# Loading a layer's weights ahead of the second tile's activations in the feed-forward groups of an attention and quantized-FFN kernel

## What is computed

```python
def _dequant(q, scale):
    return (q / 7.5 - 1.0) * repeat(scale, 16, axis=1)

def _qlora_linear(x, q, scale, bias, la, lb):
    base = einsum('btd,od->bto', x, _dequant(q, scale)) + bias
    return base + einsum('btr,or->bto', einsum('btd,rd->btr', x, la), lb)

h = x
for blk in range(3):
    y = _qlora_linear(h, qweights[2*blk], ...)
    y = gelu(_layernorm(y, ...))
    y = _qlora_linear(y, qweights[2*blk+1], ...)
    h = y + h
out = _layernorm(x + h)
```

## Time and profile before

| | us |
|---|---|
| median of two timed runs | 2959.98 (2907.43 to 3012.53) |
| the profiled execution | 2838.79 |
| its span, from first to last instruction on the slowest core (7) | 2837.3 |
| spans of the eight cores | 2818.8 to 2837.3 |
| TensorE busy with matmuls (58% of the span) | 1633.2 |
| VectorE (DVE) busy | 1037.6 |
| ScalarE (ACT) busy | 990.2 |

### The profile page before, as it was taken

How to read it: one execution, slowest core, us unless ns; L and a number is a source line. 1 busy time by engine, 2 the same in 40 slices (tenths; PEclk the granted TensorE clock), 3 DMA queues, 4 the chain that set the end, 5 groups by cost and what they waited for, 6 DMA issues and landing times.

```text
span 2837.3 us, 21874 instructions; the slowest of 8 cores (2818.8 to 2837.3 us)
## 1 busy us (share of the span) xinstructions
PE 1633.2 (58%) x6880; PEld 681.6 (24%) x6880; DVE 1037.6 (37%) x1049; ACT 990.2 (35%) x1472; POOL 54.3 (2%) x100
## 2 busy tenths in 40 slices
PE   0899880199987011115765545685457655456853
PEld 0344330044433000002322222232123222222321
DVE  2113435212343644441452604236314526042362
ACT  0321121042213012114446435544444464355444
POOL 0000000000000000100000000000000000000000
PEclk9999995599998555557888868897578888678975
DMA  5210123420021466673010050100230100401001
GB/s 169 79 60 16 45 74 148 163 81 32 16 75 45 176 219 212 226 235 110 30 34 26 15 163 30 60 30 0 92 116 30 31 29 14 164 30 60 30 1 60
DMA packets 72543, 228.63 MB, mean 81 GB/s; under 512 B 6768, under 2 KB 7024, under 8 KB 66032
## 3 DMA queue, kind: packets, MB, share of 16 engines
q1 hardware_dynamic: 61680, 181.09, 19.7%
q0 software_dynamic: 10752, 46.14, 4.1%
HBM read 181.07 MB, written 46.14 MB: 80 GB/s over the span
## 4 chain that ended last, share of the span: by engine, by line
PE 46%; ACT 16%; DMA 13%; DVE 12%; issue 7%; PEld 2%; DVEq 1%; SPq 1%; PEldq 1%; ACTq 0%; POOL 0%; POOLq 0%
PE ps L745 23%; PE ps L258 8%; DMA PL<-sc_t 5%; PE ps L370 4%; PE ps L313 4%; ACT PL L921 2%; PE ps L725 2%; PE ps L973 2%; DMA PL<-wq_t 2%; PEld ps L446 2%; DMA PL<-weffs 2%; DMA PL<-xt 2%; DVE PL L913 2%; DVE PL L911 2%; PE ps L727 1%
## 5 line engine op out<-in xcount | busy, mean ns | idle before, releaser
L745 PE MATMUL ps<-PL 128*128 128x512 bf16 x3072 | 724.4, 392 | 400.5 <-ACT PL L921 308.7
L745 PEld LDWEIGHTS ps<-PL 128*128 128x128 bf16 x3072 | 305.8, 100 | 793.9 <-issue 456.7
L258 PE MATMUL ps<-PL 128*128 128x512 bf16 x1024 | 226.3, 384 | 212.4 <-DVE PL L211 209.1
L889 DVE TENSOR_TENSOR e2s<-e2s,m2s 128x512 f32<-128x512 f32 x32 | 22.1, 691 | 625.9 <-ACT e2s L881 625.9
L617 PE MATMUL ps<-PL 32*128 32x512 bf16 x48 | 28.1, 586 | 302.6 <-DVEq L640 179.0
L258 PEld LDWEIGHTS ps<-PL 128*128 128x128 bf16 x1024 | 100.6, 99 | 337.5 <-issue 220.7
L768 ACT ACTIVATE PL<-ps,fb 128x512 bf16<-128x512 f32 x192 | 132.3, 689 | 140.8 <-PE ps L727 140.6
L781 DVE SCALAR_TENSOR_TENSOR PL<-ps,fb,PL 128x512 f32<-128x512 f32 x192 | 144.2, 751 | 94.6 <-PE ps L745 94.3
L973 PE MATMUL ps<-eye,PL 128*128 128x128 f32 x256 | 90.8, 439 | 139.4 <-ACT PL L987 74.0
L446 PE MATMUL ps<-PL 128*128 128x512 bf16 x640 | 142.7, 387 | 20.2 <-ACTq L171 20.2
L370 PE MATMUL ps<-PL 128*128 128x512 bf16 x640 | 141.1, 382 | 7.0 <-issue 4.3
(11 more groups left out here) (74 smaller groups left out, 1606.5 us busy)
## 6 DMA issues: line engine op xcount, KB each, us to landing
PL<-weffs SPq DMA_DIRECT2D x24, 2048.0 KB, 9.3
PL<-xt SPq DMA_DIRECT2D x32, 1024.0 KB, 5.7
PL<-qw_t SPq DMA_DIRECT2D x48, 512.0 KB, 5.0
PL<-sc_t SPq DMA_DIRECT2D x48, 512.0 KB, 6.3
x1s<-PL POOLq DMA_DIRECT2D x16, 1024.0 KB, 4.2
PL<-x1s SPq DMA_DIRECT2D x64, 256.0 KB, 6.7
out<-PL POOLq DMA_DIRECT2D x32, 512.0 KB, 3.0
weffs<-PL POOLq DMA_DIRECT2D x48, 256.0 KB, 6.3
```

Source lines behind the costliest of these rows:

```text
L258: last = e.matmul(ps[bank][:], bfv(area + c * 512, 1024)[:, s * 128:(s + 1) * 128], xtbf[:, c * 2048 + tc * 512:c * 2048 + (tc + 1) * 512] ...
L745: last = e.matmul(ps[bank][:], bfv(WSL[sl], 8192)[:, c * 1024 + s * 128:c * 1024 + (s + 1) * 128], src_mv[:, c * 512:(c + 1) * 512], start ...
```

## The change

In `emit_group`, the order in which SP issues the loads at the start of each group. Before: tile t0, tile t1, matrix 0, matrix 1. Now: tile t0, matrix 0, matrix 1, tile t1. The waits that each load carries are the same, as are the streams of PE, DVE, ACT and POOL.

```diff
             for j in (0, 1):
                 if hook:
                     hook(j)
-            for t in ts:
-                xm[t] = x1_load(t, (ex_x1 or {}).get(t, ()))
+            xm[ts[0]] = x1_load(ts[0], (ex_x1 or {}).get(ts[0], ()))
             wl[0] = w_load(0)
             wl[1] = w_load(1)
+            for t in ts[1:]:
+                xm[t] = x1_load(t, (ex_x1 or {}).get(t, ()))
             for t in ts:
                 cm[t] = cast_in(t, IBASE[t % 2], xm[t],
                                 extra=(ex_cast or {}).get(t, ()))
```

## The result

The change makes the kernel faster: the ratio to before is 0.9766, with a 95% interval of 0.9753 to 0.9779. The working said 0.9764, 67 us less than 2838.79; the median is now 2776.14 us, where that sum had given 2772. The number on record, 2890, is nevertheless wrong by 114 us: I had carried the ratio over to 2959.98, the median of two runs. In some executions of this program the cores of one half of the chip, or of both, run at a lower granted clock and end later; both of those runs, by their times, were such, and the ratios here leave such runs out. Six further runs of before took 2837.22 to 2847.96 us, median 2840.66, like the profiled execution. The gain on them is 66 us by the ratio.

The account below looks back on a forecast made before the run. Bound taken: PE's 91.8 us of waiting for weights at four group starts. 58.0 + 9 = 67 us off 2838.79 gives 2771.8, ratio 0.9764; carried to the two runs' median 2959.98, the forecast is 2890 us, range 2760 to 2940.

Parts of the forecast that it names:

- The four waits: PE idle for weights before the feed-forward matmuls at each group start: 29.92, 21.67, 20.12 and 20.09 us, all on the path.
- Part 1: Starts of groups 2 to 4: PE goes from t1's transposes straight into the matmuls; 61.0 less 3 for the store, 58.0 us.
- The store's delay: At each later boundary, t0's last output store lands later beside the weights: 1 us taken, between nothing and 3 us.
- the 2.6 us of room: Later boundaries: matrix 0 reckoned to land at 1656.3, 2.6 us early, with PE in t1's transposes until 1658.95.
- Part 2: Start of group 1: matrix 0 issued at 1265.1 instead of 1275.19, PE starts sooner; 9 us gained, between 7 and 11.
- another microsecond: Group 1: possible cost of the dequantization's last loads and stores sharing the DMA engines with the weights.
- Part 3: t1's loads behind the weights: cost 0, margin 6.5 us at later boundaries; in group 1 hidden, possibly with nothing to spare.
- The clock: Start of each group, first matmuls at 1.2 GHz: an earlier rise could win up to 2.4 us each; nothing taken.
- The starved store: Rival, chance 0.17 in two forms: t0's last store lands only with a weight matrix; gain 15 or 31 us.
- The falling clock: Rival, chance 0.05: TensorE granted less in the layers' long matmul stretches; with two tenths slowed, 72 us lost, 3035.
- a sooner clock: Rival, chance 0.10: clock rises sooner at three later starts, 2.4 us each; gain 74 us, ratio 0.974, 2883.
- The sum on the profiled execution: Whole kernel: 58.0 + 9 = 67 us less than 2838.79, giving 2771.8, ratio 0.9764.

Follow-up runs that it names:

- the dummies: Added to the change: one plain matmul with unread result behind each of t1's last twelve transposes in groups 1 to 3; ratio to before 0.9767.
- two further edits: On the change: separate output area for t1 (0.9789 alone) and both weight loads ahead of t0 in groups 2 to 4 (0.9758 alone); together 0.9677.
- the own buffer: On the change: t1's transposes copied into t0's dead h area, so ACT waits for no store of t0; ratio to before 0.9789.

## Why the prediction was right or wrong

**What bounds the kernel: right.** The four waits were on the path in full, and the wait that went, 67.7 us on the mean core, came out as 69.0 us between the end of the dequantization and the end of the kernel, 65.8 of the whole span.

**Part 1, groups 2 to 4: right.** Predicted 58.0 us, measured 58 with these groups alone (ratio 0.9796, 50 to 66 us by its interval, so that so close a hit is partly luck). The idle time went whole, the cast was in time (1642.18 in the changed kernel), and PE started behind the last transpose. Two terms in it were off. The store's delay, taken as 1 us per boundary, was 0.1 us on the mean of all cores; the slowest core's store took 0.5 to 1.2 us longer than that of the slowest core before. And matrix 0 was reckoned to land 16.3 us after its issue; on that core it took 15.4 to 19.1, so that the 2.6 us of room shrank to 1.0, and on one core in eight it came 1.85 us late at one start.

**Part 2, group 1: right within its bounds.** Predicted 9 us between 7 and 11; the wait fell by 8.0 us over eight cores, and the kernel with this group alone gained 8.5. By its two parts: matrix 0 is issued 9.8 us sooner (10.1 predicted), and the first matmul comes 17.3 us behind that issue where it was 15.5 before, both on the mean of the cores, against the 14.7 to 16.6 us that I used. Leaving matrix 1 out behind it changed nothing, taking t0's loads away ahead of it gave 2.7 us: what stands ahead in the queue counts. It does not explain the 1.8 us by which the landing grew, for before, t1's eight loads stood directly ahead of matrix 0 just as t0's do now. What is new beside it are the last loads and stores of the dequantization, for which the prediction allowed another microsecond; no run takes them apart, so this stays open.

**Part 3, t1: right.** In the first group its cast ended at 1296.39 + 2.29 = 1298.68, and its matmuls came at 1306.28, 22.6 us behind t0's: a margin of 7.6 us where I had feared none at one end of the range. At the start of group 2 its cast ended at 1669.66 and its matmuls came at 1676.50, a margin of 6.8 where 6.5 was reckoned. DVE's timeline of the changed kernel, group 1:

```profile
1275.81 2.29 DVE L703 CAST PL<-PL 128x4096 bf16<-128x4096 f32 x1 [4.74 <-DMA PL<-x1s]
1296.39 2.29 DVE L703 CAST PL<-PL 128x4096 bf16<-128x4096 f32 x1 [18.29 <-DMA PL<-x1s]
```

**The clock: right in the main.** Transposes did not raise it: a window of the kernel before, 2016.5 to 2028.5 us, shows PE busy with them for 11.26 of 12 us at 0.50, where the plain matmuls among the transposes brought it up. The term put at nothing was 0.4 us a start.

```profile
2016.50:2028.50 12.00, 11.26 (x26) 4.52 (x25) 4.36 (x1) 6.55 (x25) 1.59 (x3) 0.50 0.33 132
```

**The rivals.** The starved store is refuted by its own measure, ACT's wait for `out`, 8.65 us where 20 would have proved it. The falling clock did not come: L745 was busy 724.9 us in place of 724.4. The full 2.4 us of a sooner clock, or nearly, came only with the dummies.

**The step that failed** is the last of the sum: "The metric is their median, so I carry the ratio over: 2959.98 x 0.9764 = 2890." The sum on the profiled execution, 2771.8, is 4.3 us from the measured median. The two timed runs were 69 and 174 us above that execution, no row showed why, and I let them move the number all the same. They also disagreed with each other by 105 us, more than the whole effect, which should have told me that their median said little of the kernel. In their place six further runs put the kernel before at 2840.66 us in the median, 1.9 us from the profiled execution; the ratio, 0.9764, was met by 0.9766.

## What to carry to other kernels

A queue that issues loads in order makes each wait everybody's wait: put what is free to go ahead of what must wait for a late event, here 4 MB of weights ahead of a tile whose area was still in use. When such a wait is removed, look how far behind the next path is, and what the next edit puts beside it; here it was 1 to 4 us behind on the slowest core, and so two further edits that gave nothing one by one gave 25 us together. And where timed runs disagree among themselves by more than the effect, keep the sum on the execution whose rows it was made from.

## What the runs showed of the hardware

**Cores in pairs differ in how fast their loads land.** With the own buffer, matrix 0 lands 14.6 to 17.1 us after its issue at the three later starts on cores 0, 3, 4 and 6, and 19.1 to 23.8 us on cores 1, 2, 5 and 7: of each pair 0-1, 2-3, 4-5, 6-7 one is quick and one slow. PE's wait for weights, summed over the four starts, is 35.3, 37.5, 38.3 and 36.4 us on the first four, and 52.7, 58.6, 53.5 and 54.8 us on the others. The rows of L745 on core 4 of that kernel:

```profile
core 4 of [0, 1, 2, 3, 4, 5, 6, 7], span 2741.5 us
...
  DMA PL<-weffs: 38.3, 4
```

Core 5 has 53.5 us in the same row, and a span of 2764.9.

The time is that of the slowest core, so this is why that kernel gained nothing: its quick cores span 2738.8 to 2747.5 us and its slow ones 2763.9 to 2772.3, where the profiled execution of the change has 2755.9 to 2759.3 on the even cores and 2765.5 to 2773.6 on the odd ones. Which of a pair is quick is not fixed: in another execution of the change core 4 spans 2770.3 us and core 5 2759.6. The slow one is also the one that comes second: at the start of group 2 with the own buffer its matrix 0 is issued 5.2 to 9.6 us after its neighbour's. Whether it lands late because it comes second, and what the two share, was not tried.

**The clock rises with plain matmuls, and then holds for transposes.** PE 94% busy with f32 transposes for 12 us stayed at 1.2 GHz; with every second instruction a plain matmul it reached 2.4 GHz (granted 0.64 from 1650 to 1655 us with PE busy 4.94 of 5, and 1.00 from 1655 to 1660), and transposes in between ran faster too, 0.27 to 0.30 us instead of 0.42. The plain matmuls also closed PE's last gaps; which of the two counts was not taken apart. The Trainium skill (TensorE: Matmul & The Clock Gate, "Part 4: PE-mode transpose") says that the full clock does not engage for transposes; the trace agrees for transposes alone and adds that they run faster once plain matmuls have brought the clock up.
